# A new order for the last third of the front: batch 0's moments split on ScalarE, batch 3's weights rounded before the residual additions

## The reference, cut to what matters

```python
def _smooth_quant_linear(x, w):          # x: [512, D], w: [O, D]
    s = jnp.sqrt(jnp.maximum(jnp.max(jnp.abs(x), axis=0), EPS) / jnp.maximum(jnp.max(jnp.abs(w), axis=0), EPS))
    xs, ws = x / s, w * s
    x_scale = jnp.maximum(jnp.max(jnp.abs(xs), axis=-1, keepdims=True), EPS) / 127.0
    w_scale = jnp.maximum(jnp.max(jnp.abs(ws), axis=-1, keepdims=True), EPS) / 127.0
    x_q, w_q = jnp.clip(jnp.round(xs / x_scale), -127, 127), jnp.clip(jnp.round(ws / w_scale), -127, 127)
    return x_q @ w_q.T * x_scale * w_scale.T

def xattn(x, gate_up, down):             # for each of 4 batches: x [512,512], gate_up [512,512], down [512,256]
    gate, up = jnp.split(_smooth_quant_linear(x, gate_up), 2, axis=-1)
    return _smooth_quant_linear(jax.nn.silu(gate) * up, down)

def ffn(h):                              # 2048 tokens, 8 experts, DFF 2048
    logits = h @ gate_w.T
    _, sel = jax.lax.top_k(logits.sum(axis=0), 2)          # two experts for all tokens
    rw = jax.nn.softmax(logits[:, sel], axis=1)
    y = gelu(einsum('nd,kdf->knf', h, w1[sel]) + b1[sel]) ; y = einsum('knf,kfd->knd', y, w2[sel]) + b2[sel]
    return einsum('nk,knd->nd', rw, y)

x = x + xattn(layernorm(x), side, ctx)
x = x + ffn(layernorm(x))
```

## Time and profile before

| | before |
|---|---|
| median of 3 runs | 820.6 us |
| the runs | 820.12, 820.6, 821.82 us |
| span of the profiled execution | 818.7 us |
| TensorE matmul busy | 771.5 us (94%) |
| mean granted TensorE clock | 0.979 of full |

### The profile page before, as it was taken

One profiled execution on the slowest core, in us unless ns is written; L12 is line 12 of the kernel. 1 busy time (PEld: TensorE's weight loads), 2 busy tenths in 40 slices (PEclk: granted clock), 3 DMA queues, 4 the chain that ended last, 5 costly groups with the idle time before them and its releaser, 6 DMA issues.

```text
span 818.7 us, 11342 instructions
## 1 busy us (share of the span) xinstructions
PE 771.5 (94%) x3570; PEld 624.1 (76%) x3577; DVE 477.7 (58%) x669; ACT 354.6 (43%) x660; POOL 449.7 (55%) x497
## 2 busy tenths in 40 slices
PE   5688666999999999999999999999999999999998
PEld 4666455688788888888888888888888888888886
DVE  5999759797754545454545454545454545454545
ACT  3967588743442434343424343434343434242422
POOL 1789997157564646464646464646464646464622
PEclk9899968999999999999999999999999999999999
DMA  9400000301010101010101010101010101010022
GB/s 344 173 2 1 1 0 2 129 1 51 1 52 1 51 0 49 3 50 2 48 4 51 1 45 6 42 9 44 7 41 11 36 15 36 15 32 19 0 103 104
DMA packets 19077, 32.34 MB, mean 39 GB/s; under 512 B 872, under 2 KB 11240, under 8 KB 18160
## 3 DMA queue, kind: packets, MB, share of 16 engines
q1 hardware_dynamic: 18896, 31.98, 11.1%
q10 hardware_dynamic: 160, 0.08, 0.0%
HBM read 27.87 MB, written 4.19 MB: 39 GB/s over the span
## 4 chain that ended last, share of the span: by engine, by line
PE 83%; POOL 8%; DVE 3%; issue 2%; ACT 2%; DMA 1%; ACTq 0%; POOLq 0%; DVEq 0%
PE slot L805 42%; PE slot L792 34%; PE slot L850 3%; POOL wv L366 2%; POOL xf L383 1%; PE slot L667 1%; POOL wv L372 1%; POOL cv L366 1%; PE slot L585 1%; DVE rmax L1226 1%; DMA b_rows<-in_L_ffn_b 1%; POOL rstd L340 1%; POOL h_lo L476 1%; DVE stats L1217 1%; DVE peak_x L1226 1%
## 5 line engine op out<-in xcount | busy, mean ns | idle before, releaser
L792 PE MATMUL slot<-xo,a_hi 128*128 128x512 f32 x840 | 259.1, 390 | 0.0
L1541 DVE SCALAR_TENSOR_TENSOR res<-slot,rw,res 128x512 f32<-128x512 f32 x256 | 178.5, 750 | 130.3 <-PE slot L805 130.2
L1570 DVE TENSOR_TENSOR e<-slot,e 128x512 f32<-128x512 f32 x150 | 103.8, 692 | 173.4 <-PE slot L792 173.3
L805 PE MATMUL slot<-w_hi,h_hi 128*128 128x512 f32 x512 | 201.3, 393 | 0.4 <-POOL h_lo L476 0.4
L805 PE MATMUL slot<-w_lo,h_hi 128*128 128x512 f32 x512 | 199.6, 390 | 0.0
L805 PE MATMUL slot<-w_hi,h_lo 128*128 128x512 f32 x512 | 199.4, 390 | 0.0
L792 PEld LDWEIGHTS slot<-xo,a_hi 128*128 128x128 f32 x840 | 157.4, 188 | 33.3 <-DVE e L1570 0.2
L476 POOL TENSOR_TENSOR h_lo<-e,h_hi 128x512 fp32r<-128x512 f32 x96 | 138.1, 1451 | 55.0 <-ACT e L1104 54.0
L792 PE MATMUL slot<-xo,a_lo 128*128 128x512 f32 x420 | 163.7, 390 | 0.0
L805 PEld LDWEIGHTS slot<-w_hi,h_hi 128*128 128x128 f32 x512 | 96.1, 188 | 25.1 <-POOL h_lo L476 5.6
L476 POOL TENSOR_TENSOR h_lo<-hid,h_hi 128x512 fp32r<-128x512 f32 x32 | 44.1, 1378 | 124.7 <-ACT hid L1104 124.7
(11 more groups left out here) (145 smaller groups left out, 814.5 us busy)
## 6 DMA issues: line engine op xcount, KB each, us to landing
raw<-in_L_ffn_w SPq DMA_DIRECT2D x32, 512.0 KB, 3.4
res<-in_x SPq DMA_DIRECT2D x4, 1024.0 KB, 11.9
wv<-in_fside_BxS2xS SPq DMA_DIRECT2D x4, 1024.0 KB, 12.8
out_x<-res SPq DMA_DIRECT2D x3, 1024.0 KB, 3.9
cv<-in_ctx SPq DMA_DIRECT2D x4, 512.0 KB, 13.1
out_x<-res SPq DMA_DIRECT2D x4, 256.0 KB, 2.7
b_row<-in_L_ffn_b SPq DMA_DIRECT2D x2, 256.0 KB, 4.6
b_rows<-in_L_ffn_b ACTq DMA_DIRECT2D x1, 64.0 KB, 6.0
```

The costliest lines, as they stand in the source:

```text
L792: last = t.matmul(dst, a[:, i, k, :], xo[tp][:, v, k, :], start=(start and n == 0), stop=(n == 3 * H - 1), skip_group_check=True)
L805: last = t.matmul(y_bank[j][:, :], a[:, i, j * P:(j + 1) * P], v[:, f, :], start=(start and n == 0), stop=(not start and n == 2), skip_gro ...
L1541: v.scalar_tensor_tensor(out=r, in0=y_bank[j][:, :], scalar=rw[:, ds(p, 1), n:n + 1].rearrange("p a b -> p (a b)"), in1=r, op0=ALU.mult, o ...
L1570: v.tensor_tensor(dst[:, :], src, other[:, :], ALU.add).then_inc(comb_ready, 1)
```

## The change

Six things move; no arithmetic is added or taken away.

1. ScalarE: `moments(0, 2)` becomes `means` (sums and mean) and `variances` (squares and variance). Between them now stand `integers_w(2, 2, 0)` and `round_x(3, 2)`.
2. ScalarE: `normalise(0, 2)` goes behind batch 3's integers and scale row; `normalise(1, 2)` goes behind both `keep_full` of batch 0.
3. GpSimd: `round_weight(3, 2)` and both `row_scale(3, 2, ...)` come ahead of batch 1's second residual addition and of `inv_std(0, 2)`; batch 2's normalisation is cut in two around `inv_std(3, 2)`.
4. GpSimd to VectorE: the residual addition of slabs 2 and 3 of batch 1 moves to VectorE (`add_late_residual(1)`).
5. VectorE: `row_inverse(3, 2, 1)` now stands behind both `dequant(2, 2, ...)`; `normalise_last` stands ahead of `keep_lo(0, 0)` and `keep_lo(1, 0)`.
6. TensorE: `normed2(0, 0)` goes behind `product(3, 2, ...)`.

```diff
@@ VectorE, which additions it makes
-            def add_last_residual():
-                emptied(f"p2.{B - 1}.1")
+            def add_late_residual(b):
+                emptied(f"p2.{b}.1")
                 for j in range(H, TT):
-                    r = res[:, (B - 1) * TT + j, :]
-                    v.tensor_tensor(r, r, wv[B - 1][:, j, :], ALU.add).then_inc(res_last, 1)
+                    r = res[:, b * TT + j, :]
+                    v.tensor_tensor(r, r, wv[b][:, j, :], ALU.add).then_inc(res_late[b], 1)
@@ VectorE, moments
-                    if c == 2 and b == B - 1 and j >= H:
-                        dve.wait_ge(res_last, j - H + 1)
+                    if c == 2 and b in res_late and j >= H:
+                        dve.wait_ge(res_late[b], j - H + 1)
@@ TensorE
-            normed2(0, 0)
             product(3, 2, 0)
             product(3, 2, 1)
+            normed2(0, 0)
             normed2(0, 1)
@@ VectorE's list
             dequant(1, 2, 0)
+            row_inverse(3, 2, 0)
             dequant(1, 2, 1)
-            row_inverse(3, 2, 0)
             scale_w(3, 2)
-            row_inverse(3, 2, 1)
             dequant(2, 2, 0)
             dequant(2, 2, 1)
+            row_inverse(3, 2, 1)
+            add_late_residual(1)
             moments(1, 2)
```

More of the change, by code:

```diff
@@ L226, in xattn_ffn @@
         hi_ready, lo_ready = each("hi_ready"), each("lo_ready")
-        res_last, xn_last = sem("res_last"), sem("xn_last")
+        res_late, xn_last = {1: sem("res_late1"), 3: sem("res_late3")}, sem("xn_last")
         part_ready, tok_ready, t4_sum = each("part_ready"), sem("tok_ready"), sem("t4_sum")
@@ L391, in add_residual, with normalise @@
                     g.tensor_tensor(r, r, wv[b][:, j, :], ALU.add).then_inc(res_added[b], 1)
-            def normalise(b):
+            def normalise(b, h):
                 pool.wait_ge(nmr_ready[b], 2)
-                for j in range(TT):
+                for j in range(H * h, H * h + H):
                     g.tensor_scalar(xv[b][:, j, :], res[:, b * TT + j, :], rstd[1][b][:, j:j + 1], nmr[1][b][:, j:j + 1],
@@ L456, in _ @@
             round_weight(2, 2)
+            row_scale(3, 2, 0)
             smooth_weight(3, 2)
-            row_scale(3, 2, 0)
             add_residual(1, 0)
+            row_scale(3, 2, 1)
+            round_weight(3, 2)
             inv_std(0, 2)
-            row_scale(3, 2, 1)
-            add_residual(1, 1)
-            round_weight(3, 2)
             add_residual(2, 0)
+            add_residual(2, 1)
             inv_std(1, 2)
-            add_residual(2, 1)
             add_residual(3, 0)
             inv_std(2, 2)
-            normalise(2)
+            normalise(2, 0)
             inv_std(3, 2)
+            normalise(2, 1)
             pool.sem_inc(sums_ready, 4)
@@ L903, in summed, with means @@
                 act.wait_ge(mom_link, sums[0])
-            def moments(b, c):
+            def means(b, c):
                 if c == 1:
@@ L914, in moments, with variances @@
                 summed(s.mul(nmean[c - 1][b][:, :], mv[b][:, :, 0], -1.0 / D))
+            def variances(b, c):
                 for j in range(TT):
@@ L1011, in _ @@
             normalise(1, 1)
-            moments(2, 1)
+            means(2, 1)
+            variances(2, 1)
             keep_smooth_row(0, 1)
-            moments(3, 1)
+            means(3, 1)
+            variances(3, 1)
             normalise(2, 1)
@@ L1066, in _ @@
             keep_scale_row(2, 2)
-            moments(0, 2)
+            means(0, 2)
             integers_w(2, 2, 0)
             round_x(3, 2)
-            normalise(0, 2)
+            variances(0, 2)
             integers_x(3, 2, 0)
@@ L1073, in _ @@
             keep_scale_row(3, 2)
+            normalise(0, 2)
             keep_full(0, 0)
+            keep_full(0, 1)
             normalise(1, 2)
-            keep_full(0, 1)
             keep_full(1, 0)
@@ L1493, in _ @@
             moments(2, 2)
-            add_last_residual()
+            add_late_residual(3)
             moments(3, 2)
+            normalise_last()
             keep_lo(0, 0)
             keep_lo(1, 0)
-            normalise_last()
             token_sums(2)
```

## The result

| | before | after |
|---|---|---|
| median of 20 runs each, side by side | 820.24 us | 821.92 us |
| span of the profiled execution | 818.7 us | 820.7 us |
| ratio of the times, after to before | | 1.002 (95% interval 1.0013 to 1.0027) |

The change makes the kernel 1.7 us slower. The forecast was 819.7, 0.9 us faster than the 820.6 then known, with a range of 819.0 to 821.3 (818.3 to 821.4 for 8 chances in 10). One run of after, at 1572.68 us, was in a disturbed state and is left out of the ratio; the other 19 lie between 821.36 and 823.37 us. The profile of after is of an execution that took 822.66 us, 0.7 above the median.

A forecast was written before the change was run, and what follows sets the result against it. Only the front had room, its chain running through GpSimd's inverses; with 2 us of slack, ScalarE would become the bound. 820.6 - 0.15 (order) - 0.8 (clock) = 819.65, say 819.7 us; range 819.0 to 821.3.

The forecast's parts named there:

- 0.8 from the clock: TensorE's tail: half clock begins at some 128 us, ends up to 6 us earlier; 0.8 us gained, middle of 0 to 1.6.
- the sum of ScalarE's waits: ScalarE up to its last rounding: four waits, together 2.9 to 3.7 us, taken as 3.7.
- (1): ScalarE, through with batch 3's token integers, waits for TensorE's transposes of the rounded weights: 1.0 to 1.5 us.
- (2): ScalarE at `keep_full(0, 0)`, directly behind `normalise(0, 2)`, waits for the last two transposes: 0.2 to 0.5 us.
- (3): ScalarE at `keep_full(0, 1)` waits while TensorE refills slot 0, which both halves of batch 0 use: 1.2 us.
- (4): ScalarE at `keep_full(1, 0)` waits for the last transposes of batch 1: 0.5 us.
- the sign of being wrong: On GpSimd, a rounding of batch 3's weights later than 119 would show the forecast wrong.
- Half clock reaches into the router: Router groups run at half clock, some 1.6 us each for one to two groups: 822.1 to 823.7 us; chance 0.10.
- the sign that was to decide for it: TensorE's granted clock still low at 146 us would decide for half clock in the router.
- ScalarE doesn't become the bound: ScalarE's four waits come to 2 us, batch 3 is normalised at 137.1: gain 1.8 us, 818.8 us; chance 0.04.
- The order does less than it says: GpSimd's rounding waits over 1.4 us for the inverse, passed into ScalarE's first wait; price 0.7 us, no separate chance.
- The clock comes back early: TensorE's clock doesn't fall or returns before the dense tail: 1.6 to 2.4 us gained, say 818.4 us; chance 0.25.

The follow-up runs named there:

- the rounding alone: After plus one wait: VectorE begins batch 1's late addition only when all of batch 3's weights are rounded; 820.92 us, ratio 1.0016 to before.
- the run with full clock: After with TensorE's idle time filled in eight places by identity transposes that nothing reads; 819.86 us, ratio 1.0001 to before.
- the kept-busy run of before: Before with TensorE's idle time filled in four places by identity transposes that nothing reads; 821.69 us, ratio 1.0010 to before.
- the kernel with the swap: After with `normalise(1, 2)` again between the two `keep_full` of batch 0 on ScalarE; 819.28 us, ratio 0.9991 to before.
- the swap and one piece: After with `normalise(1, 2)` between batch 0's `keep_full` halves and batch 2 normalised whole on GpSimd ahead of `inv_std(3, 2)`; 819.27 us, ratio 0.9991 to before.

## Why the prediction was wrong

**What held.** ScalarE became the bound: no wait for GpSimd ahead of batch 3's normalisation, whose `nmr` was ready at 137.40, 1.50 us earlier than before (2.36 counted from batch 0's sums; forecast 3.2). ScalarE's work stayed the same (30.84 - 5.56 = 25.28 us; forecast 25.16). Batch 2's product came 2.2 us earlier. GpSimd waited at its rounding for the inverse (1.28 us; forecast 1.3), and the wait between the two `keep_full` of batch 0 was 1.18 (forecast 1.2).

**What was met by luck.** The tail is 0.72 us shorter, where the forecast had 0.8 from the clock. But the half clock did not begin once at about 128 and end by 142. It fell three times, the last time from 143.42 to 146.84, later than the 145.69 at which it ended in before. It covered 3.42 us of the tail instead of 6.76.

**The step that failed** is the sum of ScalarE's waits: 5.56 us measured, 3.7 forecast. Wait by wait:

| wait | forecast | measured | what was missed |
|---|---|---|---|
| (1) batch 3's weight integers | 1.0 to 1.5 | 2.10 | the rounding beside VectorE's addition; 1.47 with the rounding alone |
| (2) batch 0's first half | 0.2 to 0.5 | 1.06 | product at half clock; 0.53 at full |
| (3) batch 0's second half | 1.2 | 1.18 | nothing |
| (4) batch 1's first half | 0.5 | 0.78 | transposes at half clock; 0.53 in the run with full clock |
| (5) batch 1's second half | none | 0.44 | the same; 0 in the run with full clock |

The surplus is 0.60 + 0.56 - 0.02 + 0.28 + 0.44 = 1.86 us. A third of it is the rounding's duration, which the prediction took from the earlier trace rows as 1.86 us although the change itself puts an addition of VectorE's on the same microsecond. The rounding began at 119.05, the sign of being wrong that the prediction had named (later than 119), but 0.86 us of that is the later start; what counted was its length. The warning stood in the timeline of before. The inverse of 1.97 us in the earlier trace rows ran beside VectorE's `keep_lo`, and another of the same shape did not:

```profile
116.72 1.04 POOL L340 TENSOR_TENSOR rstd<-var_e,neg_half 128x4 f32<-128x4 f32 x1
```

The Trainium skill, "SBUF — State Buffer", section "Who interferes with whom", says that a VectorE instruction with two inputs in SBUF contends with a GpSimd instruction that reads SBUF, and that the order of issue decides which of the two blocks. The trace agrees: VectorE's addition came first and kept its 1.26 us, and of the rounding instructions one took 1344 ns and three 480.

The other two thirds, 0.56 + 0.28 + 0.44 = 1.28 us, go with the clock. The prediction let the half clock begin at about 128 us, where "little is lost"; it fell on 122.94 to 126.36 and 133.18 to 136.60, under the product and the transposes for which a bound ScalarE waits. Before was bound by GpSimd, and there half clock under batch 2's product had been covered, as the kept-busy run of before shows. So half clock goes with about 1.3 us of loss in the region, against 0.72 of gain in the tail, where the forecast had 0.8 of gain alone. The 1.25 us between after and its kept-busy version, counted from the rounding on, fit this, but the fills are a change of their own, so the clock's share is a reading of profiles and not shown by an experiment that moves the clock alone. Where the clock falls differs between executions (at 122.94 in after, at 128.40 in the kernel with the swap, whose program is the same up to some 127 us), so the 1.3 us is this one profile's.

The forecast's difference to before's profile was -0.95 us, the measured one is +1.97. Of the 2.92 us between them the waits are 1.86, the later start of the sums 0.86 (most likely chance, as is where in the region the half clock fell), small steps 0.12 and the tail 0.08.

**The rivals.** "Half clock reaches into the router" gives a time near the measured one, but by another mechanism: the clock was indeed still low at 146 us, the sign that was to decide for it, but the chain has 2.18 us for the first router group where before's has 2.79, and the tail became shorter. It was low at 146 because all had come later. "ScalarE doesn't become the bound" was false. "The order does less than it says" had the right path, a later rounding that goes into ScalarE's first wait, but for another reason: GpSimd waited 1.28 us for the inverse, within the 1.4 allowed, and the rounding itself was long. "The clock comes back early" fell too; the longest idle stretch of TensorE behind 110 us did shrink, to 2.15 us, and the clock still fell three times. The Trainium skill, "TensorE: Matmul & The Clock Gate", section "HAM oscillation", gives the avoidance of long idle gaps as the rule; by it alone the clock should have stayed, and the measurement speaks against that. No rival was the collision of two engines inside the change.

**What the change is worth, then.** The swap takes away, first of all, wait (3), which the forecast had priced rightly: it shows what the order costs, not what the forecast missed. With this one swap on ScalarE it is 2.6 us better, and neither slower nor, clear of the noise, faster than before. The versions that mend one thing more, without fills, end at 819.2 to 819.5, which the times don't tell apart from the swap alone, and each profile has a different latecomer (ScalarE, GpSimd's second half, VectorE's `keep_lo`). Open stays how the 2.6 us divide, and why the runs of after spread less than those of before (2.0 against 4.1 us).

## What to carry to other kernels

When a change hands the bound from one engine to another, price the new bound's waits with the durations that hold there, not with those of rows in which the work was covered: in before a product at half clock cost nothing, and in after ScalarE waited for one. Before an operation moves from GpSimd to VectorE, look at what GpSimd runs in the same microsecond. And where two refills of one buffer follow each other on the engine that binds, keep a long instruction group between them: here these two lines moved the median by 2.6 us, while the rest of the change is not clear of the noise.

## What the runs showed of the hardware

- GpSimd and VectorE slow each other in both directions. Beside VectorE's fp32 addition from SBUF a rounding instruction of GpSimd took 1344 instead of 480 ns; beside GpSimd's addition VectorE's 128x4 variance step took 1.25 us instead of 0.16 (rows at 123.04 and 135.87 of VectorE's timeline in after), and its addition 2.31 instead of 1.26 us (before with the addition on VectorE, at 121.96); beside `keep_lo` the 128x4 inverse took 1.97 us instead of 1.00.
- The half clock's place moves between executions with the same instructions ahead of it. The kernel with the swap and the one with the swap and one piece are the same program up to some 132 us; in one profile the clock fell at 128.40, in the other at 121.17.
- Short idle pieces are no guarantee of full clock. In before with TensorE kept busy, the clock fell from 138.80 behind work whose idle pieces were 1.50, 0.25, 0.31 and 1.35 us.
